# u's upper half behind the first scaling of A on ScalarE, its lower half ahead of the inputs' normalisation on VectorE, in a kernel of two fused passes

## What is computed

```
Mn = Wn @ inorm(x) + bn;  Mm = Wm @ inorm(ctx) + bm
A  = softmax(Mn^T Mm)                      # 512 x 512 per batch
x1 = Wo @ ((Wl @ ctx + bl) @ A^T) + bo + x # 128 x 512 per batch
q  = layer_norm(x1) @ q_w + q_b;  k, v = ctx @ k_w + k_b, ctx @ v_w + v_b
hidden = softmax(q k^T / sqrt(32), 16 heads) v @ cproj_w + cproj_b + x1
out = hidden + gelu(layer_norm(hidden) @ fc_w + fc_b) @ proj_w + proj_b
```

## Time and profile before

| what | value |
|---|---|
| median of 3 runs | 3034.93 us |
| lowest, highest | 3034.04, 3037.51 us |
| profiled execution, its own time | 3036.39 us |
| its span, first to last instruction | 3034.5 us |
| TensorE busy | 2864.3 us (94%) |
| VectorE, ScalarE, GpSimd busy | 1910.4 (63%), 1469.5 (48%), 1119.3 us (37%) |
| stretch 200 to 1400 us: TensorE, VectorE, ScalarE, GpSimd busy | 1134.3, 1086.6, 959.2, 792.7 us |

### The profile page before, as it was taken

One profiled execution on the slowest core, in us unless ns is written; L12 is line 12 of the kernel. 1 busy time (PEld: TensorE's weight loads), 2 busy tenths in 40 slices (PEclk: granted clock), 3 DMA queues, 4 the chain that ended last, 5 costly groups with the idle time before them and its releaser, 6 DMA issues. The chain is left out here.

```text
span 3034.5 us, 54536 instructions
## 1 busy us (share of the span) xinstructions
PE 2864.3 (94%) x17527; PEld 2369.3 (78%) x17527; DVE 1910.4 (63%) x3705; ACT 1469.5 (48%) x4210; POOL 1119.3 (37%) x998
## 2 busy tenths in 40 slices
PE   5899999999999999999977999999999999999999
PEld 3777777777777777777765888888888888888887
DVE  5799899999989899999855433333333333333332
ACT  5788778887878877888743211111111111111111
POOL 5566666666666666666632000000000000000000
PEclk7999999999999999999997999999999999999999
DMA  6588888888888888888863210101111111011110
GB/s 184 164 237 230 231 238 229 239 229 235 232 227 237 228 235 236 232 235 232 226 175 129 69 40 17 41 28 41 41 41 41 29 27 39 30 41 41 41 28 14
DMA packets 440889, 416.65 MB, mean 137 GB/s; under 512 B 155200, under 2 KB 319552, under 8 KB 440768
## 3 DMA queue, kind: packets, MB, share of 16 engines
q1 hardware_dynamic: 440768, 415.40, 49.4%
HBM read 231.79 MB, written 167.77 MB: 132 GB/s over the span
## 5 line engine op out<-in xcount | busy, mean ns | idle before, releaser
L1306 ACT ACTIVATE gl<-pre,fc_bias 128x512 f32<-128x512 f32 x256 | 176.6, 690 | 1119.4 <-PE pre L1391 1119.4
L1345 DVE CAST hT_hi<-gl 128x512 fp32r<-128x512 f32 x256 | 109.3, 427 | 840.2 <-ACT gl L1306 840.2
L673 ACT ACTIVATE rows<-bank,negmax 128x128 f32<-128x128 f32 x1024 | 364.2, 394 | 209.2 <-DVE negmax L829 198.9
L599 POOL TENSOR_TENSOR at_lo<-a_blocks,at_hi 128x512 fp32r<-128x512 f32 x256 | 335.4, 1330 | 190.1 <-ACT at_hi L710 190.1
L590 POOL TENSOR_TENSOR rows<-rows,rsum 128x512 f32<-128x512 f32 x256 | 266.0, 1040 | 271.4 <-DVE rsum L825 271.4
L177 POOL TENSOR_TENSOR rstd<-ve,neghalf 128x4 f32<-128x4 f32 x16 | 16.3, 1018 | 870.9 <-DVE ve L171 870.9
L1390 PE MATMUL pre<-yT_hi,rest_lo 128*128 128x512 f32 x768 | 298.9, 389 | 0.0
L1389 PE MATMUL acc<-rest_lo,hT_hi 128*128 128x512 f32 x768 | 298.9, 389 | 0.0
L1391 PE MATMUL acc<-rest_hi,hT_hi 128*128 128x512 f32 x768 | 298.9, 389 | 0.0
L1391 PE MATMUL pre<-yT_hi,rest_hi 128*128 128x512 f32 x768 | 298.8, 389 | 0.0
L1389 PE MATMUL pre<-yT_lo,rest_hi 128*128 128x512 f32 x768 | 298.8, 389 | 0.0
(11 more groups left out here) (158 smaller groups left out, 7886.1 us busy)
## 6 DMA issues: line engine op xcount, KB each, us to landing
a_turn<-rows SPq DMA_DIRECT2D x128, 512.0 KB, 7.6
a_blocks<-a_turn SPq DMA_DIRECT2D x256, 256.0 KB, 5.0
p_turn<-rows SPq DMA_DIRECT2D x128, 512.0 KB, 4.5
p_blocks<-p_turn SPq DMA_DIRECT2D x256, 256.0 KB, 5.9
x_ctx<-in_x SPq DMA_DIRECT2D x64, 256.0 KB, 2.6
x_ctx<-in_ctx SPq DMA_DIRECT2D x64, 256.0 KB, 2.9
blocks<-in_ctx SPq DMA_DIRECT2D x256, 64.0 KB, 5.5
small<-in_x SPq DMA_DIRECT2D x64, 256.0 KB, 5.9
```

Of the source, the lines that this page charges most:

```text
L599: pool.tensor_tensor(by_rows(at_lo, j), a_chunks[:, j], by_rows(at_hi, j).bitcast(F32), ALU.subtract).then_inc(at_lo_set, 1)
L673: act.activation(probs[:, :, r, c, :], by_chunk(S1_BANK[r])[:, c, :].rearrange("p (d b) -> p d b", b=32), ACT.Exp, bias=negmax1[:, r, c:c ...
L1306: act.activation(gl[:, i % 2, :], pre[i % 2][:], ACT.Gelu_apprx_tanh, bias=mlp.fc_bias[:, i:i + 1]).then_inc(gelu_done, 1)
```

## The change

ScalarE: L738's four scalings become a helper, `scale_a(t)`. The first is issued where all four stood, then u's upper half, then the other three. VectorE: u's lower half, with its wait, goes from behind the last two turns of A to ahead of the inputs' normalisation. No instruction is added or removed, and the order on TensorE, GpSimd and SyncE stays.

```diff
@@ ScalarE, slot(s)
+                def scale_a(t):
+                    if b0.exists():
+                        act.activation(A[:, :, t, :], A[:, :, t, :], ACT.Identity,
+                                       scale=rsum0[:, t:t + 1]).then_inc(a_scaled, 1)
...
                 if b0.exists():
                     act.wait_ge(rsum0_set, b0.nth(1, 1))
-                    for t in range(DC):
-                        act.activation(A[:, :, t, :], A[:, :, t, :], ACT.Identity,
-                                       scale=rsum0[:, t:t + 1]).then_inc(a_scaled, 1)
+                scale_a(0)
                 if b1.exists():
                     act.wait_ge(u_done, b1.nth(1, 1))
                     act.activation(u_hi, bank[U_BANK][:], ACT.Copy).then_inc(u_hi_set, 1)
+                scale_a(1)
+                scale_a(2)
+                scale_a(3)
                 upper_at(0)
                 upper_at(1)
                 qk_bias(1)
@@ VectorE, slot(s)
                 if b5.exists():
                     dve.wait_ge(outT_hi_set, b5.nth(1, 1))
                     lower(outT_lo, bank[PV_BANK][:], outT_hi, outT_lo_set)
+                if b1.exists():
+                    dve.wait_ge(u_hi_set, b1.nth(1, 1))
+                    lower(u_lo, bank[U_BANK][:], u_hi, u_lo_set)
                 if ahead.exists():
...
                 turn_a(2)
                 turn_a(3)
-                if b1.exists():
-                    dve.wait_ge(u_hi_set, b1.nth(1, 1))
-                    lower(u_lo, bank[U_BANK][:], u_hi, u_lo_set)
```

## The result

The changed kernel takes **3052.30 us** (median of 4 runs, 3044.69 to 3056.75); the kernel before, beside it, 3035.59 (3034.04 to 3037.51). The ratio is 1.0055, 95% interval 1.0043 to 1.0068: **slower, by 16.7 us**. That is outside my range (3030 to 3050) and on the side to which I gave 0.38.

A forecast was written before the change was run, and what follows sets the result against it. It took a scaling-to-scaling chain over GpSimd and x1n, without u, as the bound. 6.2 - 1.8 - 1 + 1 = +4.4 us on the profiled 3036.4 gives 3040.8; the runs' median lies 1.5 below: 3039 us, range 3030 to 3050.

The forecast's parts named there:

- the side to which I gave 0.38: Whole kernel: the change makes it slower, by more than 6.1 us; chance 0.38.
- What bounds the kernel: Attention pass: a chain from scaling to scaling, 23.63 us, without u; x1n's normalisation ends 0.28 us after L629.
- the ring: Attention pass: scaling, at_hi, normed_hi, GpSimd's normed_lo to ctxT_lo, x1n, turn, maxima and sums, next scaling; 23.63 us.
- Parts 1 and 3: VectorE's u_lo goes earlier, delaying L913 by 0.58 us, at no cost; TensorE's wait goes, regular slots gain 0.
- Part 2: ScalarE waits 0.22 us for U before u_hi in 28 slots: +6.2 us (5.0 to 8.1).
- Part 4: One disturbed slot, where late blocks delayed u_lo and TensorE stood 1.83 us, is gone: -1.8 us.
- Part 5: Last slots, without a next input: 0.5 us gained in each of two, -1 us (0 to -1.2).
- Part 6: SP's queue comes 0.58 us later, A's blocks have 0 to 1.2 us to spare: +1 us (0 to +15).
- The play: Turns of A, ahead of ScalarE: a turn that stalls up to some 0.6 us costs nothing.
- Rival C: VectorE's L913 meets GpSimd's at_lo, 0.9 us each; in one slot of five 10 us, 3049; chance 0.05.
- B: A's way through DRAM closes a ring of its own; 0.2 us a slot puts 11 us on top, 3050; chance 0.22.

The follow-up runs named there:

- The swap: Kernel before with GpSimd's second L614 moved behind x1b: 3032.65 us, ratio 0.9992; with an early u as well: 3003.80 us, ratio 0.9890.
- hi_only: Changed kernel with u's lower half back behind the last turns, upper half still behind the first scaling: 3040.33 us, ratio 1.0015.
- lo_behind_norm: Changed kernel with u's lower half behind the inputs' normalisation, ahead of A's last two turns: 3036.89 us, ratio 1.0003.
- write_first: Changed kernel with SyncE issuing A's write ahead of the next inputs' load: 3033.41 us, ratio 0.9992.
- hi_after_two: Changed kernel with u's upper half behind the second scaling of A instead of the first: 3053.01 us, ratio 1.0057.

## Why the prediction was wrong

- **What bounds the kernel: right.** u isn't in the ring. The end of x1n stayed at the end of L629 plus 0.28 in every slot, 12.24 us behind the first scaling where ScalarE doesn't wait and 12.42 where it does (12.28 before). The swap shows the ring from outside: only with GpSimd's part shorter does an early u pay.
- **Parts 1 and 3 (VectorE's move, TensorE's wait): right.** 62.8 us of waits went to 0.6 and gave nothing, since x1n was next; the regular slots didn't change by it.
- **Part 2 (ScalarE's wait): right, a little high.** 0.22 forecast, 0.18 measured, in every second slot; 6.2 against 5.0, and 4.5 in hi_only.
- **Part 4 (the disturbed slot): no use as a term.** That slot went, and others came. Single disturbances in one profile are a sample: before has six in the middle. Nor was its price all u_lo's: before has two slots with the first turn at 0.57 us, and the one whose granted clock stayed at 1.00 lasts 24.0 us, this one, with 3.4 us at 0.50, 25.5.
- **Part 5 (the last slots): right.** -1 forecast, -1.5 in the profile.
- **Part 6 is the step that failed**, "a few slots in 56 pay some tenths: +1 us". The trigger was read well: the blocks were said to have 0 to 1.2 us to spare, 0.6 in the middle; the records give 0.02 to 1.53, mean 0.70, and 0.24 after the change. The play was even larger than I said, 0.76 us (0.87 - 0.11) against 0.6. But beyond the play I put tenths, and there stands a step of 2.5 us: 1.2 for the hold with what queues behind it, 1.2 for TensorE's half clock.
- **Rival C had the mechanism and the wrong price.** I computed that L922 and at_lo would be 0.4 us apart and that a stall could close it, priced the meeting at 0.9 us (what L851 loses beside GpSimd) and gave it 0.05. The hold itself is 1.1 us, near that. What I left out is what queues behind it: the turns, at_hi, normed_hi, GpSimd's ring, and then the mask and TensorE's clock. And I held B and C for two cases, where B's late blocks are what triggers C. The Trainium skill (SBUF — State Buffer, section "SBUF: two separate sides") states the lock that is at work here, and the trace agrees: L922 takes 1653 ns at its longest beside at_lo and 531 otherwise. On who goes first the trace is less plain than the page, which gives the ports to the one that starts first: the held L922 is recorded from 825.63 us, 0.08 us ahead of at_lo (825.72), while the L922 ahead of it still ran.
- **B in its pure form didn't come.** VectorE waited for the blocks 18 times in 1200 us, and 14 of those cost nothing; the other four are the long slots.

By its own terms the sum would have been 5.0 - 1.5 + 4 x 2.5 = +13.5, less the 3.9 that before lost in its own disturbed slots: +9.6, against +8.3 in the profiled execution. The range ended at 3050 because no slower case in it had a price of more than 0.9 us for an event. The other half of the median's +16.7 lies in runs without a profile and stays open; that it goes the same way is shown only by lo_behind_norm and write_first, which take it away with the long slots.

## What to carry to other kernels

Price an instruction that is moved later by the whole queue behind it up to the next shared resource, and look for a step: slack that absorbs a delay up to some point says nothing of the cost past it. When a long wait is removed and nothing is gained, look for the chain that ties with it and try both edits together before giving either up: here 4.7 and 2.8 us apart made 31.7 together. And when a transfer closes a ring, ask first what is issued ahead of it: the order of a few DMA issues was worth 32 us once the rest was out of the way.

## What was not expected of the hardware

- VectorE's mask, 0.21 us in most slots (L945), took 0.75 beside GpSimd's L614, and up to 1.30; before the change, where it came later in the slot, its median was 0.75:

```profile
L939 DVE TENSOR_SCALAR mask_less<-mask_u x51: 295/748/1150, 209.6 to 1393.5; 128x128 bf16<-128x128 uint8 x51
```

```profile
L945 DVE TENSOR_SCALAR mask_less<-mask_u x50: 208/210/1304, 210.1 to 1380.5; 128x128 bf16<-128x128 uint8 x50
```

  So an instruction can be three times as long by its place alone, and a small operand's too.
- An idle time of TensorE of 2.07 us was followed, 1.4 us later, by 3.4 us at a granted clock of 0.50, in which a matmul of 512 columns came every 0.43 us instead of 0.23. The turn of x1n then started 1.3 us after x1n was done, instead of 0.14. Nearly the same idle time (2.04 to 2.13 us) left the clock at 1.00 in five slots of hi_after_two and cost nothing there; the same trace puts the clock's price at 1.2 us a slot.
- The same write of A lands 2.9 us after its issue with the loads of x and ctx and the read of p behind it, and 7.8 with them ahead of it. So here a transfer's time to landing depends on what is issued just ahead of it.
